# Plain attention: who issues the transfers that place the query rows

## What is computed

```python
xn = layernorm(x)                                   # (8, 512, 256)
# the first branch takes xn in its own layout: (8, 512, 256)
q = (xn @ Wq + bq).reshape(B, T, 16, 16)            # 16 heads of 16 features
k = (xn @ Wk + bk).reshape(B, T, 16, 16)
v = (xn @ Wv + bv).reshape(B, T, 16, 16)
scores = einsum('bqhd,bkhd->bhqk', q, k) * 16 ** -0.5
probs = softmax(scores, axis=-1)
attn = einsum('bhqk,bkhd->bqhd', probs, v).reshape(B, T, 256) @ Wo + bo
y = layer_norm(xn + attn, ln1_g, ln1_b)             # then a router and 4 experts, each token by one
```

## Time and profile before

| what | value |
|---|---|
| median of 3 runs | 2044.2 us |
| lowest and highest of the runs | 2033.72 and 2051.11 us |
| the profiled execution's own time | 2037.85 us |
| its span, from the first to the last instruction | 2036.1 us |
| mean granted TensorE clock | 0.942 of full speed |
| busy, of the span: PE, DVE, POOL, ACT | 87%, 64%, 48%, 41% |
| DMA queue q1 (SP's): bytes, share of the 16 engines | 119.63 MB, 23.9% |
| DMA queue q10 (ACT's): bytes, share | 0.26 MB, 0.1% |

### The profile page before, as it was taken

How to read it: one execution, slowest core, us unless ns; L and a number is a source line. 1 busy time by engine, 2 the same in 40 slices (tenths; PEclk the granted TensorE clock), 3 DMA queues, 4 the chain that set the end, 5 groups by cost and what they waited for, 6 DMA issues and landing times.

```text
span 2036.1 us, 31873 instructions
## 1 busy us (share of the span) xinstructions
PE 1776.4 (87%) x11505; PEld 1053.3 (52%) x11506; DVE 1293.8 (64%) x2864; ACT 835.9 (41%) x1144; POOL 978.6 (48%) x630
## 2 busy tenths in 40 slices
PE   4989998998983059999479999999999999999998
PEld 2333334333332059999344655646556465554654
DVE  5777777777762427777566665666656566565761
ACT  2555555664551124444135153351533415334152
POOL 1213254244235534454438457384573846737464
PEclk7889999999997579999679999999999999999999
DMA  7516624642610626654400010100001000010000
GB/s 113 62 41 117 101 40 94 108 57 71 107 40 24 228 100 226 227 208 166 103 11 1 11 33 1 42 1 17 26 1 42 1 21 22 1 42 1 22 11 11
DMA packets 73471, 130.02 MB, mean 64 GB/s; under 512 B 11350, under 2 KB 50422, under 8 KB 68476
## 3 DMA queue, kind: packets, MB, share of 16 engines
q1 hardware_dynamic: 70012, 119.63, 23.9%
q0 software_dynamic: 3072, 8.39, 1.3%
q10 hardware_dynamic: 256, 0.26, 0.1%
HBM read 76.09 MB, written 26.74 MB: 51 GB/s over the span
## 4 chain that ended last, share of the span: by engine, by line
PE 43%; POOL 3%; DVE 3%; issue 1%; ACT 1%; DMA 0%; POOLq 0%; DVEq 0%; SPq 0%
PE a_psO L716 11%; PE a_psS L702 11%; PE a_psO L739 6%; PE a_psM L676 5%; PE a_psS L664 4%; PE a_psS L648 3%; PE a_psS L729 3%; POOL a_k_tok L349 1%; POOL a_q_tok L349 1%; ACT a_probs L467 1%; DVE a_junk L533 1%; POOL a_oT L372 1%; DVE a_alibi L610 0%; DVE a_qL L523 0%; DVE a_probs L503 0%
## 5 line engine op out<-in xcount | busy, mean ns | idle before, releaser
L384 POOL TENSOR_TENSOR a_probs<-a_probs 128x1024 f32<-128x1024 f32 x144 | 341.7, 2399 | 300.2 <-PE a_psO L716 300.2
L533 DVE CUSTOM_DVE_ANT_0 a_junk<-a_psM,a_alibi 128x512 bf16<-128x512 f32 x512 | 333.3, 689 | 198.9 <-PE a_psM L676 195.6
L1258 DVE TENSOR_REDUCE f_n_tok<-f_psR 128x1 f32<-128x512 f32 x512 | 326.8, 682 | 131.3 <-PE f_psR L1399 130.3
L467 ACT ACTIVATE a_probs<-a_psS 128x1024 f32<-128x1024 f32 x256 | 248.9, 1024 | 271.9 <-PE a_psS L702 271.1
L1202 ACT ACTIVATE f_probs<-f_psS 128x1024 f32<-128x1024 f32 x256 | 248.0, 1023 | 190.0 <-PE f_psS L1418 187.9
L716 PE MATMUL a_psO<-a_probs,a_v 128*32 128x512 f32 x2048 | 244.0, 597 | 0.0
L1399 PE MATMUL f_psR<-f_kP,f_qP 48*128 48x512 f32 x512 | 171.5, 519 | 52.6 <-DVE f_n_tok L1258 38.6
L1399 PEld LDWEIGHTS f_psR<-f_kP,f_qP 48*128 48x128 f32 x512 | 65.9, 193 | 237.8 <-issue 108.8
L676 PE MATMUL a_psM<-a_kH,a_qH 64*128 64x512 f32 x512 | 122.7, 474 | 29.4 <-DVE a_n_tok L533 29.4
L1431 PE MATMUL f_psO<-f_probs,f_v 128*32 128x512 f32 x1024 | 141.8, 627 | 0.6 <-ACT f_probs L1202 0.6
L739 PE MATMUL a_psO<-a_wo,a_oT 128*128 128x256 f32 x512 | 127.3, 395 | 4.4 <-POOL a_oT L372 4.4
(11 more groups left out here) (190 smaller groups left out, 3505.6 us busy)
## 6 DMA issues: line engine op xcount, KB each, us to landing
w_w_high<-w_parts SPq DMA_DIRECT2D x19, 1024.0 KB, 5.1
w_w_low<-w_parts SPq DMA_DIRECT2D x19, 1024.0 KB, 7.1
f_kP<-f_high SPq DMA_DIRECT2D x64, 128.0 KB, 5.7
f_qP<-f_high SPq DMA_DIRECT2D x64, 128.0 KB, 7.7
e_xs<-sorted_x SPq DMA_DIRECT2D x19, 256.0 KB, 2.7
sorted_z<-e_z SPq DMA_DIRECT2D x19, 256.0 KB, 2.2
sorted_x<-f_zeros SPq DMA_DIRECT2D x7, 640.0 KB, 13.2
f_xn<-in_L_attn_x SPq DMA_DIRECT2D x8, 512.0 KB, 3.9
```

What stands on the lines that cost most here:

```text
L384: nc.gpsimd.tensor_tensor(slots, slots, probs[:, first - GRP:first - GRP + 2, :], ALU.add).then_inc(added.sem, 1)
L467: nc.scalar.activation(probs[:, slots, :], psS[:, 2 * p:2 * p + 2, :], ACT.Exp).then_inc(exp_done.sem, 1)
L533: nc.vector.tensor_tensor_reduce(out=junk[:, a, :], in0=psM[:, a, :], in1=alibi[:, h, :], scale=1.0, scalar=-3.0e38, op0=ALU.add, op1=ALU.max,
L1258: nc.vector.tensor_reduce(n_tok[:, c, column:column + 1], psR[:, ring_bank("max", u), :], AX.X, ALU.max, negate=True).then_inc(max_done.se ...
```

## The change

The body of `move_sides` becomes a function `move_rows(queue, b, g, i)` that moves one kind of rows, i = 0 for keys and 1 for queries, and issues on the engine that it is given. SP issues the rows of keys in all batches, and those of queries for batch 0 alone. For batch b+1, ScalarE issues the queries' transfers of the half g = 0 at the end of its period (1, 2), and those of g = 1 at the end of its period (2, 0). The waits and the number of transfers (six for each kind, half and batch) are as before.

```diff
+        def move_rows(queue, b, g, i):
+
+            former = divmod(2 * b + g - 3, 2)
+            if former[0] >= 0:
+                queue.wait_ge(score_ps.sem, score_ps.at(former[0], QP * (2 * former[1] + 2) * TT - 1))
+            pair_rows, kinds = ((kP, (high, low, high)), (qP, (high, high, low)))[i]
+            n = 2 * g + i
+            queue.wait_ge(low_done.sem, low_done.at(b, n))
+            first_place = place_of(b, HP * g)
+            for a in range(2):
+                for k, part in enumerate(kinds):
+                    first = FB * a + FH * k
+                    queue.dma_start(pair_rows[first:first + FH, first_place:first_place + HP, :].bitcast(F32),
+                                    part[FB * a:FB * (a + 1), n, :].bitcast(F32)).then_inc(moved[g].sem, 16)
+
...
             def move_sides(b, g):
-
...
-                for i, (pair_rows, kinds) in enumerate(((kP, (high, low, high)), (qP, (high, high, low)))):
...
+                move_rows(sp, b, g, 0)
+                if b == 0:
+                    move_rows(sp, b, g, 1)
...
                         elif kind == "maxima" and present(b, kind, n):
                             take_maxima(b + belongs(kind, n), n)
+                    if more and (quad, j) in ((1, 2), (2, 0)):
+                        move_rows(act, b + 1, quad - 1, 1)
```

More of the change, by code:

```diff
@@ L984, in move_sides @@
             def move_sides(b, g):
-                former = divmod(2 * b + g - 3, 2)
-                if former[0] >= 0:
-                    sp.wait_ge(score_ps.sem, score_ps.at(former[0], QP * (2 * former[1] + 2) * TT - 1))
-                for i, (pair_rows, kinds) in enumerate(((kP, (high, low, high)), (qP, (high, high, low)))):
[L990 to L997, removed]
+                move_rows(sp, b, g, 0)
+                if b == 0:
+                    move_rows(sp, b, g, 1)
             def load_w1(n):
```

## The result

The changed kernel takes 2067.72 us (median of 4 runs, 2059.93 to 2074.79) where the kernel before takes 2041.4 (4 runs, one more than in the table above, 2033.72 to 2051.11). The ratio is 1.0127, with a 95% interval of 1.0071 to 1.0184: slower by 26 us. Measured again beside the experiments it was 1.0100 (1.0065 to 1.0135). The profiled execution of it took 2068.15 us, with a span of 2066.4.

What follows compares the result with a forecast made beforehand. TensorE was taken to bound the phase, its scores waiting for ScalarE's exponentials. Waits of 6 x 3.3 + 2 us plus 3.4 us of clock make 25 us: from the median 2044.2 to 2069 us, 1.2% slower, range 2046 to 2092.

Steps and rivals of the forecast that it cites:

- the chain of the waits: TensorE's lateness from period 8 to period 12: 3.3 us in each of six batches, 2 us in batch 0.
- three signs that were to show it wrong: Issues overlapping ScalarE's activations, rows of quad 3 landing as early as before, or the clock falling in each batch.
- What SP saves is worth nothing: Twelve issues fewer per batch, 7.7 us of SP's stream, gain nothing because nobody waits for SP's issuing.
- TensorE's scores wait for ScalarE: TensorE's scores at 163.96, 168.30, 172.68 and 182.07 wait for exponentials, so ScalarE's delay beyond its idle time reaches TensorE.
- Six issues hold ScalarE for 3.8 us: Behind periods 6 and 8, issues delay exponentials: period 8 late 1.8 us, batch 2.2 in all; bounds 0.7 to 4.
- The maxima's rows land behind the queries of g = 1: On ScalarE's queue, quad 3's rows land at 184 to 186; period 12 late 3.3 us, replacing the 2.2; bounds 2.2 to 4.
- `moved[0]` is covered: Queries of g = 0 are there at 172.9, TensorE asks at 174: no cost, 1 us to spare.
- The clock: New waits of about 2 us bring two more clock falls in seven batches at 1.7 us each: 3.4 us, none to 12.
- only the issues cost: Rival, chance 0.27: maxima's rows land in time, a batch loses 0.7 to 2.2 us; 2049 to 2059 us.
- all covered: Rival, chance 0.10: ScalarE's issues fit the gaps and the maxima's rows come in time; 2044 us.
- Heavier: Rival, chance 0.13: queries of g = 0 land after 174, each batch waits twice, clock falls in each; 2093 us.
- Faster: Rival, chance 0.05: TensorE's waits for maxima's rows at 163.96 and 182.07 go, 1.4 us a batch; 2034 us.

Runs made afterwards that it cites:

- e9: The changed kernel timed again, unaltered, beside the other experiments: 2060.24 us, 1.0100 of the kernel before.
- e4: The kernel before, SP moving everything, plus six 64-byte transfers issued by ScalarE at each of the change's two places: 2057.07 us, 1.0055 of the kernel before.
- e2: The changed kernel with only the queries of g = 1 issued by ScalarE, those of g = 0 by SP: 2061.12 us, 1.0071 of the kernel before.
- e3: The changed kernel with ScalarE issuing the queries of g = 1 at the end of period (3, 0), behind the maxima's rows: 2049.02 us, 1.0016 of the kernel before.
- e7: The changed kernel with SP's stores, load and clearing moved behind the load of the next rows: 2060.61 us, 1.0083 of the kernel before.
- e11: The changed kernel, but ScalarE issues only g = 1's queries, behind the maxima's rows at period (3, 0); SP issues g = 0's: 2032.31 us, 0.9951 of before.
- e10: The kernel before with unused TensorE multiplications ahead of periods 12 (6) and 14 (10, behind an added wait): 2032.48 us, 0.9939 of the kernel before.

## Why the prediction was right, and where its terms were off

The forecast, 2069 us and 1.2% slower, came out (2067.7 and 1.27%, and 1.00% in e9). That it came out so closely is luck: the chain of the waits was counted about twice too long and the clock far too cheap, and the two errors cancelled. Of the three signs that were to show it wrong, two appeared: ScalarE's issues overlap its activations, and the clock fell in each batch. The third did not: the rows of quad 3 landed late, as forecast.

*What SP saves is worth nothing.* Right for the sum. The wait for the rows of quad 2 ahead of period 8 (0.56 us) no longer shows, but a longer one for exponentials stands in its place (0.89 and 0.41 us), in e4 too, where SP issues everything.

*TensorE's scores wait for ScalarE.* By their semaphores they do, but the working read more into its four times than they show: in the kernel before none of them waited for exponentials. Period 8 (163.96) and period 12 (182.07) waited for the maxima's rows, and the exponentials ahead of period 12 are those of period 11, which aren't among the ones named.

*Six issues hold ScalarE for 3.8 us.* Right in length: from 159.07 to 163.21 and from 167.93 to 171.73, 4.1 and 3.8 us; the first group's last issue took 0.88 while SP issued too. Wrong in the start: they begin ahead of the instruction in front of them. That was the end of the range that no row showed, and the rows after show it. So period 8 is late by 1.0 and not by 1.8 us, and the second group costs 0, not 0.4: 1.0 us in place of 2.2.

*The maxima's rows land behind the queries of g = 1.* The mechanism was right, and e2, e3 and e7 bear it out. In batch 1 the last query lands at 184.0 (forecast 183 to 185.6), and TensorE waits 2.12 us (forecast about 2) and goes on at 184.4 (forecast 185.4). It is late by 2.2 us, not by 3.3, since only 1.0 us of the step before carries over; and batch 1 has the longest of these waits.

*`moved[0]` is covered.* Right, with more to spare: the queries of g = 0 land at most 7.7 us after their issue, by 170.1, and no wait for them shows.

*The clock.* This term was mis-sized: 3.4 us, with bounds of none and 12. Of the 31 us between the two profiles TensorE was idle for 10.9 and busy for 20.1 longer, on the same instructions: the waits cost 11 us, and 20 went with the clock. I had counted two falls more, at 1.7 us each. In the changed kernel the clock fell behind the wait of period 12 in all seven batches, for two before, and in five of them again ahead of period 8 of the next batch, in a stretch where the change puts no wait at all. Added up over windows of 10 us, the lower of its two levels, 1.2 GHz of 2.4, held for 27 us of the phase before and for 79 after. The price was low as well: 20.1 us for these 52 are 0.39 each, where the earlier trace rows gave 1.7 us for the 8.2 us that 0.59 of a window makes, 0.21 each.

So in these two executions the chain of the two waits was counted as 22 us and measured as 11, and the clock was counted as 3.4 and measured as 20. Over many executions the clock is a smaller part, but more than half: the runs of e9 have a median of 0.933 for 0.9385, and at 18 us for 0.01 that is about 10 of the 17 us between the medians (an estimate from the clocks and times of all runs, not a separate measurement). e7 says that this part doesn't belong to the one wait: without most of the waits at period 12 the clock fell elsewhere.

Of the rivals, *only the issues cost* is refused by e2 and *all covered* by e4. *Heavier* failed since `moved[0]` was in time, though two things that it said, that each batch waits twice and that the clock falls in each, did come about. *Faster* came true only where the change was altered (e11).

## What to carry to other kernels

Issuing a transfer held ScalarE for 0.51 to 0.88 us, whatever its size. Put issues where the next engine has work of its own for longer than that, as at the second place and not at the first. ScalarE's queue, with small urgent transfers on it, lost its use when six large ones were put in front of them: put the large ones behind (e3, e11). A wait can cost more than itself, and not always at its own place: 11 us more of idle time came with 20 us more of work at a lower clock. So compare medians of many runs, look at the granted clock of each run, and try to fill waits with unused work (e10; it and e11 can't be told apart, and both are faster than the two kernels compared here).

## What had not been expected of the hardware

ScalarE's issue of 64 bytes takes as long as one of 128 KB: five in 3.56 us (e4), against 0.55 to 0.88 us for one large. An issue can start before the instruction in front of it in the program has begun: at 159.07 with `high` from 159.54 on, at 167.93 with the copy from 168.08 on. 128 KB from SBUF to SBUF in rows of 2 KB move at 124 GB/s, while a stretch with the stores and the clearing reached 246 GB/s on the mean:

```profile
170.00:180.00 10.00, 9.65 (x57) 4.17 (x56) 7.80 (x15) 5.63 (x7) 1.27 (x1) 1.00 1.05 246
```
